# Attention's probabilities times values: one fp32 product against three 16-bit products, with low parts made on GpSimd and VectorE

## The chip, the cores and the metric

The kernel runs on one core of a Trainium2 chip. The metric is the device time of one execution in microseconds, lower is better.

## The reference, cut to what matters

```python
# x: (32 images, 128 channels, 32 x 32), so N = 1024 positions of C = 128
def L0(x):                                    # global attention, one head, per image
    h = group_norm(x, 32 groups)
    q, k, v = split(qkv_w @ h + qkv_b)
    attn = softmax((q^T k) * C ** -0.5)       # 1024 x 1024
    return x + proj_w @ (v @ attn^T) + proj_b
x = L0(x)
t = tokens(x)                                 # (32, 1024, 128)
t = t + L1_attn(layernorm(t))                 # windows of 32, 8 heads of 16, then an MLP of 4 x 128, layer norms
t = t + L1_ffn(layernorm(t))                  # input and weights rounded to fp8, one product, bias
```

The change is in `v @ attn^T` of the first stage.

## The kernel before, in words

Each engine runs its own list of steps per turn of a loop over images. The lists stand in `PROGRAM` (line 46) as text: `pv:3-` is step pv with index 3 for the image one behind the turn's, `--` two behind, and `@5` on TensorE's list gives the PSUM bank. The order is fixed by hand or by a planner outside the file; the engines meet only through semaphores. `iterations` (line 115) gives the turns: the first four and the last two are written out, the 28 between are a hardware loop (`Fori`, line 285). `tenants` and `claim` make TensorE wait until the last holder of a bank has been read; `RELEASE` (line 96) says by which semaphore.

An image's global attention goes like this. `qg`, `kg` and `vg` (lines 902 to 916) make queries, keys and values from three 16-bit products each (`three`, line 868: high x high, high x low, low x high). The values come with the output projection folded in. `max` (line 926) is a rough product of the high parts whose row maxima VectorE takes (line 705); the maxima go through `shift` to be subtracted inside the score product. `st` (line 947), c = 0 to 15, makes the transposed scores of 128 keys x 512 queries; the half of the queries is c // 8, the key tile c % 8. ScalarE turns a score tile into p with one exponential (line 524), into a ring of four fp32 buffers `p32` (`PRING = 4`). `pv` (line 961) multiplies the four 128-query tiles of that p, as the stationary operand, with 128 x 129 values `vg32`; column 129 is ones and gives the row sum. Eight of these accumulate in two PSUM banks; VectorE then divides and adds x (line 735).

```python
last = mm(ps[:, b, at:at + PVW], p32[:, c % PRING, part], vg32[:, j, :], start=j == 0 and q % 2 == 0,
          stop=j == MT - 1, skip_group_check=True)
```

The second stage works on two halves of 512 tokens: `turn_in`, `q`, `k`, `v`, `score0`/`score1` (line 1022), softmax per window, `pv0`/`pv1` (line 1040), `out`, `turn_mid`, `up0` to `up3`, `down` (line 1072, fp32), then the third stage with `turn_q` and `ffn`. A high part is a copy to fp16 by ScalarE, its low part a subtraction by VectorE (lines 699, 760, 765, 774, 807). Layer norms take their statistics on VectorE (lines 742 to 751), the power of -0.5 on GpSimd (line 380), and the scaling on ScalarE (line 493). GpSimd also does softmax's product (line 414), rounding (422, 424) and sums with rows (398 to 440). SyncE issues the transfers that spread keys and probabilities (lines 323, 330).

## Time and profile before

| | us |
|---|---|
| three runs | 2353.22, 2352.03, 2344.88 |
| median | 2352.03 |
| the profiled execution, its own time | 2352.98 |
| its span in the profile | 2351.2 |

The profiled execution is one more run of the same program, and all rows come from it. Engines are PE (TensorE; PEld is its weight loads, which overlap), DVE (VectorE), ACT (ScalarE), POOL (GpSimd), SP (SyncE). A matmul's duration includes its way through the array, so that the price of one in a stream is the distance from its start to the next start. A group's name is output <- inputs; L976 is line 976.

### The profile page before, as it was taken

How to read it: one execution, taken by the hardware profiler on the slowest of the kernel's cores; microseconds unless marked ns; L12 is line 12 of the kernel's file. 1: busy time of each engine (PE TensorE's matmuls, PEld its weight loads, DVE VectorE, ACT ScalarE, POOL GpSimd, SP SyncE). 2: the span in 40 equal slices, each digit the busy share in tenths (PEclk: the TensorE clock that was granted, in tenths of full speed). 3: DMA queues.
4: the chain of work that ended last, by engine and by line, in shares of the span. 5: the costliest groups of instructions: out<-in, count | busy, mean ns of one | idle time of the engine just before them, and what ended most of it. 6: DMA issues, size and time to landing. Idle time of an engine off the chain costs nothing.

```text
span 2351.2 us, 62343 instructions
## 1 busy us (share of the span) xinstructions
PE 2205.4 (94%) x21902; PEld 1605.7 (68%) x21902; DVE 1753.6 (75%) x5668; ACT 1480.0 (63%) x2881; POOL 1229.4 (52%) x1323
## 2 busy tenths in 40 slices
PE   4999999999999999999999999999999999999984
PEld 3677766677776677776677776677777677767663
DVE  5677777777787777787777787777787787787753
ACT  2566666766666766666666666666666666666653
POOL 5255554555554555554555555555555555555544
PEclk8999999999999999999999999999999999999997
DMA  1111111111111111111111111111111111111110
GB/s 44 35 31 33 42 36 45 38 33 29 44 36 45 38 33 30 42 36 45 41 31 33 39 36 45 42 29 35 36 36 45 44 28 36 35 36 45 36 28 19
DMA packets 76094, 86.08 MB, mean 37 GB/s; under 512 B 20624, under 2 KB 55440, under 8 KB 76048
## 3 DMA queue, kind: packets, MB, share of 16 engines
q1 hardware_dynamic: 62368, 52.44, 9.3%
q10 hardware_dynamic: 13680, 33.04, 4.3%
q8 instruction: 28, 0.46, 0.1%
q14 instruction: 18, 0.15, 0.0%
HBM read 18.29 MB, written 16.78 MB: 15 GB/s over the span
## 4 chain that ended last, share of the span: by engine, by line
PE 72%; DVE 10%; ACT 8%; issue 4%; DMA 3%; SPq 3%; POOL 1%; ACTq 0%; DVEq 0%; POOLq 0%
PE ps L976 15%; PE ps L1072 10%; PE ps L870 9%; PE ps L872 9%; PE ps L871 9%; PE ps L957 4%; PE ps L1040 4%; ACT y L493 3%; PE ps L1022 3%; PE ps L934 2%; PE ps L988 2%; DMA ptbd<-et 2%; PE ps L923 1%; SPq L330 1%; SPq L323 1%
## 5 line engine op out<-in xcount | busy, mean ns | idle before, releaser
L380 POOL TENSOR_TENSOR rstd<-veps,halfpow 128x4 f32<-128x4 f32 x256 | 264.5, 1033 | 531.6 <-DVE veps L750 531.6
L976 PEld LDWEIGHTS ps<-vg,p 128*128 128x128 f32 x4096 | 505.6, 192 | 40.4 <-ACT p L524 6.5
L976 PE MATMUL ps<-vg,p 128*128 128x129 f32 x4096 | 523.2, 277 | 0.9 <-ACT p L524 0.9
L524 ACT ACTIVATE p<-ps 128x512 f32<-128x512 f32 x512 | 291.9, 589 | 128.1 <-PE ps L872 104.3
L705 DVE TENSOR_REDUCE cm<-ps 128x1 f32<-128x512 f32 x512 | 334.7, 680 | 16.2 <-PE ps L934 16.1
L414 POOL TENSOR_TENSOR e<-e,srec 128x512 f32<-128x512 f32 x128 | 134.3, 1049 | 243.2 <-DVE srec L793 240.2
L1072 PE MATMUL ps<-w,hid 128*128 128x128 f32 x2048 | 241.7, 276 | 1.7 <-ACT hid L576 1.7
L1072 PEld LDWEIGHTS ps<-w,hid 128*128 128x128 f32 x2048 | 236.2, 192 | 7.6 <-issue 1.8
L576 ACT ACTIVATE hid<-ps,cols 128x512 f32<-128x512 f32 x256 | 165.8, 684 | 97.7 <-PE ps L872 97.7
L934 PE MATMUL ps<-kgh,qgh 128*128 128x512 f16 x512 | 176.0, 384 | 40.6 <-DVE qgl L699 34.1
L957 PE MATMUL ps<-shift,minus 128*128 128x512 bf16 x512 | 194.5, 380 | 2.0
L870 PE MATMUL ps<-qgh,kgh 128*128 128x512 f16 x512 | 194.5, 380 | 0.0
L871 PE MATMUL ps<-qgl,kgh 128*128 128x512 f16 x512 | 194.4, 380 | 0.0
L872 PE MATMUL ps<-qgh,kgl 128*128 128x512 f16 x512 | 194.3, 379 | 0.0
L567 ACT ACTIVATE oh<-ps 128x512 f16<-128x512 f32 x64 | 38.2, 597 | 175.5 <-PE ps L1040 175.5
L398 POOL TENSOR_TENSOR y<-y,rows 128x512 f32<-128x512 f32 x64 | 81.6, 1275 | 127.4 <-PE ps L988 127.4
L760 DVE TENSOR_TENSOR xl<-ps,xh 128x512 f16<-128x512 f32 x128 | 88.5, 692 | 72.7 <-ACT xh L532 69.5
L824 DVE TENSOR_TENSOR w<-ps,res 128x512 f32<-128x512 f32 x64 | 44.3, 692 | 130.0 <-PE ps L1072 126.9
L1040 PE MATMUL ps<-ptbd,v 128*32 128x128 f32 x4096 | 134.3, 278 | 4.8 <-DMA ptbd<-et 3.3
L493 ACT ACTIVATE y<-y,nshift,rstd 128x128 f32<-128x128 f32 x256 | 105.2, 483 | 43.2 <-POOL nshift L387 43.2
L493 ACT ACTIVATE y<-t,nshift,rstd 128x128 f32<-128x128 f32 x256 | 105.5, 483 | 39.2 <-POOL nshift L387 20.1
L1040 PEld LDWEIGHTS ps<-ptbd,v 128*32 128x32 f32 x4096 | 107.5, 111 | 29.0 <-DMA ptbd<-et 22.6
(184 smaller groups left out, 5508.6 us busy)
## 6 DMA issues: line engine op xcount, KB each, us to landing
ptbd<-et SPq DMA_DIRECT2D x512, 64.0 KB, 2.1
kbd<-kk SPq DMA_DIRECT2D x512, 32.0 KB, 2.0
out_y<-o_sb ACTq DMA_DIRECT2D x64, 256.0 KB, 2.4
x_sb<-in_x ACTq DMA_DIRECT2D x31, 512.0 KB, 3.9
x_sb<-in_x SPq DMA_DIRECT2D x1, 512.0 KB, 3.4
e<-in_w_t SPq DMA_DIRECT2D x1, 256.0 KB, 3.7
w<-in_w_t SPq DMA_DIRECT2D x1, 256.0 KB, 3.7
hid<-in_in_w_t SPq DMA_DIRECT2D x1, 192.0 KB, 2.4
```

The lines of the kernel that those rows point to most:

```text
L380: g.tensor_tensor(rstd[:, k, h, :], veps[:, k, h, :], halfpow[:], ALU.pow).then_inc(s[f"ln_pow{k}"], 1)
L493: last = sc.activation(dst[:, h, P * j:P * (j + 1)] if dst is z else dst[:, h, j, :], src[:, h, j, :], ACT.Identity, bias=nshift[:, k, h, ...
L524: sc.activation(p32[:, c % PRING, :], bank("st", c), ACT.Exp, scale=C ** -0.5).then_inc(s["p_made"], 1)
L705: v_.reduce_max(cm[:, c // 2, c % 2:c % 2 + 1], bank("max", c), X).then_inc(s["max_out"], 1)
L870: mm(dst, lhi, rhi, start=first, stop=False, **kw)
L871: mm(dst, lhi, rlo, start=False, stop=False, **kw)
L872: return mm(dst, llo, rhi, start=False, stop=last, **kw)
L934: mm(bank("max", c), qgh[:, P * (c // 2):P * (c // 2 + 1)], kgh[:, HALF * (c % 2):HALF * (c % 2 + 1)], start=True, stop=True).then_inc(s[" ...
L957: mm(bank("st", c), minus[:], shift[:, h, :], start=True, stop=False)
L976: last = mm(ps[:, b, at:at + PVW], p32[:, c % PRING, part], vg32[:, j, :], start=j == 0 and q % 2 == 0, stop=j == MT - 1, skip_group_check ...
L1040: last = mm(ps[WIN * two:WIN * (two + 1), BANK["pv0", h], P * j:P * (j + 1)], v32[:, h, odd, j, WIN * two:WIN * (two + 1)], ptbd[:, h, j, ...
L1072: last = mm(bank("down", h)[:, part], hid[:, f, part], w2[:, f, :], start=f == 0, stop=f == FT - 1)
```

## The change

- pv's product is three products of 16-bit operands with the same accumulation: upper half of p x high part of vg, upper half x low part, low part x high part. The upper half is read in place: every second 16-bit word of `p32`, seen as bf16. The low part `p_lo` (fp16, a ring of four as well) is p32 minus that upper half; GpSimd makes it for c % 4 in (0, 2), VectorE for the others, in steps called `st` on their lists.
- ScalarE writes vg as fp16 (`vgh`), VectorE adds a step `vg` for the low part (`vgl`, bf16). Bank vg is released by the low part. Ones stay in column 129 of vgh, zeros in that of vgl.
- pv waits for the low part's semaphore instead of p's.
- The lists of all five engines are laid out anew, with new banks. The main loop is written out turn by turn instead of a hardware loop.

In the diff, ScalarE's and SyncE's lists are cut.

```diff
+LOW_POOL = (0, 2)
...
     "pe": """
-        max:1@1- max:2@2- max:3@0- vg:1@5- turn_in:1@3-- pv0:0@1-- max:4@2- max:5@5- k:1@4-- max:6@0- pv1:0--
-        max:7@3- turn_x:0@4- v:1@5-- out:0@2-- q:1@1-- shift:0@0- turn_x:1@3- max:8@2- st:0@4- max:9@0- st:1@3-
-        max:10@2- pv:0- score0:1@0-- max:11@5- turn_mid:0@3-- st:2@4- score1:1@0-- up0:0@2-- up1:0@3-- pv:1-
-        up2:0@2-- up3:0@1-- st:3@3- st:4@0- down:0@2-- pv0:1@0-- pv1:1-- max:12@1- st:5@5- max:13@3- max:14@2-
-        out:1@4-- st:6@0- pv:2- pv:3- st:7@1- max:15@3- pv:4- pv:5- shift:1@4- turn_mid:1@2-- pv:6- pv:7- up0:1@1--
-        up1:1@0-- up2:1@4-- up3:1@3-- st:8@5- gn1:0@4 down:1@2-- pv:8- st:9@0- turn_in:0@1- st:10@5- st:11@0- k:0@2-
-        turn_q:0@1-- st:12@3- pv:9- st:13@4- ffn:0@2-- q:0@1- st:14@0- pv:10- gn2:0@2 pv:11- st:15@2- pv:12-
-        score0:0@1- score1:0@3- pv:13- pv:14- pv:15- vg:0@5 kg:0@3 kg:1@4 qg:0@2 turn_q:1@0-- v:0@5- qg:1@1
-        ffn:1@0-- max:0@5""",
+        qg:1@0- vg:1@2- turn_in:1@1-- v:0@4-- max:2@3- max:3@5- k:1@1-- max:4@4- max:5@0- pv0:0@3-- max:6@5- pv1:0--
+        max:7@2- turn_x:1@1- q:1@0-- max:8@5- out:0@3-- shift:0@2- v:1@4-- st:0@2- st:1@0- score0:1@1-- score1:1@5--
+        st:2@3- max:9@2- max:10@4- turn_mid:0@1-- st:3@0- pv:0- max:11@5- up0:0@1-- up1:0@3-- up2:0@0-- up3:0@1--
+        st:4@4- down:0@0-- pv0:1@3-- pv1:1-- pv:1- pv:2- out:1@5-- st:5@1- max:12@4- max:13@3- max:14@5- st:6@2-
+        pv:3- st:7@1- max:15@3- pv:4- pv:5- turn_mid:1@0-- pv:6- shift:1@1- pv:7- up0:1@4-- st:8@0- up1:1@3--
+        gn1:0@5 up2:1@4-- up3:1@0-- st:9@1- down:1@5-- st:10@0- st:11@3- turn_in:0@2- pv:8- st:12@4- turn_q:0@5--
+        k:0@2- q:0@3- pv:9- pv:10- st:13@4- st:14@1- pv:11- gn2:0@2 st:15@5- pv:12- ffn:0@4-- score0:0@1-
+        score1:0@2- pv:13- kg:0@5 pv:14- pv:15- kg:1@2 qg:0@0 turn_x:0@4 turn_q:1@1-- vg:0@5 ffn:1@1-- max:0@1
+        max:1@4""",
     "dve": """
-        ln_in:1-- turn_p0:0-- turn_p1:0-- qg:0- qg:1- max:0- kg:0- max:1- max:2- kg:1- turn_in:1-- max:3- max:4-
-        max:5- k:1-- max:6- pv1:0-- max:7- maxima:0- out:0-- max:8- max:9- q:1-- max:10- score0:1-- turn_mid:0--
-        prob0:1-- score1:1-- turn_p0:1-- prob1:1-- turn_p1:1-- max:11- down:0-- pv1:1-- max:12- out:1-- max:13-
-        max:14- max:15- maxima:1- gn0:0 turn_mid:1-- ln_q:0-- pv:7- ln_in:0- quant:0-- down:1-- turn_in:0- gn1:0
-        k:0- ln_q:1-- q:0- gn2:0 quant:1-- score0:0- score1:0- prob0:0- pv:15- prob1:0-""",
+        pv:15-- kg:0- ln_in:1-- qg:0- turn_p0:0-- kg:1- max:0- vg:0- turn_p1:0-- max:1- qg:1- turn_in:1-- vg:1-
+        max:2- max:3- k:1-- max:4- max:5- max:6- max:7- pv1:0-- maxima:0- q:1-- out:0-- max:8- score0:1-- score1:1--
+        prob0:1-- turn_mid:0-- prob1:1-- turn_p0:1-- max:9- max:10- st:1- turn_p1:1-- gn0:0 max:11- down:0-- pv1:1--
+        st:3- out:1-- max:12- max:13- max:14- st:5- max:15- maxima:1- st:7- turn_mid:1-- ln_q:0-- pv:7- ln_in:0-
+        gn1:0 quant:0-- down:1-- turn_in:0- st:9- k:0- st:11- ln_q:1-- st:13- q:0- gn2:0 st:15- quant:1-- score0:0-
+        score1:0- prob0:0- prob1:0-""",
...
     "pool": """
-        prob1:1-- keep:1-- norm_mid:0-- down:0-- out:1-- norm_out:0-- norm_mid:1-- ln_q:0-- ln_in:0- quant:0--
-        down:1-- norm_out:1-- bias_out:0- ln_q:1-- gn2:0 quant:1-- prob0:0- prob1:0- ln_in:1- bias_out:1- keep:0-
-        out:0- prob0:1-""",
+        out:0-- st:0- bias_out:1-- prob0:1-- prob1:1-- norm_mid:0-- keep:0-- st:2- down:0-- st:4- keep:1-- out:1--
+        st:6- norm_out:0-- norm_mid:1-- ln_q:0-- st:8- ln_in:0- quant:0-- down:1-- st:10- norm_out:1-- st:12-
+        ln_q:1-- gn2:0 st:14- quant:1-- prob0:0- prob1:0- ln_in:1- bias_out:0-""",
...
 RELEASE = {
-    "qg": ("qg_lo", 2, False), "kg": ("kg_lo", 2, False), "vg": ("vg_made", 2, False),
+    "qg": ("qg_lo", 2, False), "kg": ("kg_lo", 2, False), "vg": ("vg_lo", 2, False),
     "turn_x": ("xt_made", 2, False), "max": ("max_out", 2 * MT, False), "shift": ("shift_made", 2, False),
...
         kgh, kgl = sb("kgh", [P, N], F16), sb("kgl", [P, N], F16)
-        vg32 = sb("vg32", [P, MT, PVW])
+        vgh, vgl = sb("vgh", [P, MT, PVW], F16), sb("vgl", [P, MT, PVW], BF16)
         cm = sb("cm", [P, MT, 2])
         p32 = sb("p32", [P, PRING, HALF])
+        p_lo = sb("p_lo", [P, PRING, HALF], F16)
+        p_hi = p32[:].bitcast(BF16)[:, :, 1::2]
         rsum = sb("rsum", [P, 2, 2])
...
             x_in x_bias gn_stats gn_mv gn_mm gn_mean gn_diff gn_var gn_veps gn_pow gn_scale gn_neg gn_coef h32_made h_hi h_lo
-            qg_mm kg_mm vg_mm turn_x_mm qg_hi kg_hi vg_made qg_lo kg_lo xt_made
+            qg_mm kg_mm vg_mm turn_x_mm qg_hi kg_hi vg_made vg_lo qg_lo kg_lo xt_made
             max_mm max_out cmax_made chi_made cparts_made shift_turned shift_made
-            st_mm p_made pv_mm rsum_made t_made
+            st_mm p_made p_low_pool p_low_dve pv_mm rsum_made t_made
             turn_in_mm turn_mid_mm x_hi x_lo q_mm k_mm v_mm
...
+        def low_by(c):
+            return "pool" if c % 4 in LOW_POOL else "dve"
+        def low_count(img, c):
+            each = [low_by(x) == low_by(c) for x in range(2 * MT)]
+            return upto(img, sum(each[:c + 1]), per=sum(each))
         def by_head(ap):
...
                 iteration(i, i)
-            with engine.Fori(loop.start, loop.stop) as i:
+            for i in loop:
                 iteration("steady", i)
...
                                 pattern=[[GROUP, P // GROUP], [0, GROUP]], channel_multiplier=-1).then_inc(s["const_mask"], 1)
-                for tile, value in ((cparts[:], 0.0), (vg32[:], 1.0), (ones, 1.0), (shift[:], 0.0)):
+                for tile, value in ((cparts[:], 0.0), (vgh[:], 1.0), (vgl[:], 0.0), (ones, 1.0), (shift[:], 0.0)):
                     g.memset(tile, value).then_inc(s["const_made"], 1)
...
+            def st(kind, img, c):
+                pool.wait_ge(s["p_made"], upto(img, c + 1, per=2 * MT))
+                if due(value := upto(img, c + 1 - PRING, per=2 * MT)):
+                    pool.wait_ge(s["pv_mm"], value)
+                at = c % PRING
+                g.tensor_tensor(p_lo[:, at, :], p32[:, at, :], p_hi[:, at, :], ALU.subtract).then_inc(s["p_low_pool"], 1)
             def quant(kind, img, h):
...
-            run(pool, "pool", {"gn2": gn2, "ln_in": power_step(0), "out": power_step(1), "bias_out": bias_out, "norm_mid": norm_mid, "keep": keep, "prob0": prob(0), "prob1": prob(1), "quant": quant, "down": power_step(2), "norm_out": norm_out,
+            run(pool, "pool", {"gn2": gn2, "st": st, "ln_in": power_step(0), "out": power_step(1), "bias_out": bias_out, "norm_mid": norm_mid, "keep": keep, "prob0": prob(0), "prob1": prob(1), "quant": quant, "down": power_step(2), "norm_out": norm_out,
                        "ln_q": power_step(3)}, prologue)
...
                 if isinstance(img, int) and img == 0 and c == 0:
-                    act.wait_ge(s["const_made"], 9)
+                    act.wait_ge(s["const_made"], 10)
                     act.wait_ge(s["pv_mm"], value)
-                sc.activation(vg32[:, HT * c:HT * (c + 1), 0:C], tiles(bank("vg", c)), ACT.Copy).then_inc(s["vg_made"], 1)
+                sc.activation(vgh[:, HT * c:HT * (c + 1), 0:C], tiles(bank("vg", c)), ACT.Copy).then_inc(s["vg_made"], 1)
...
                 if isinstance(img, int) and img == 0:
-                    act.wait_ge(s["const_made"], 9 + 2 * (1 + HEADS + HT))
+                    act.wait_ge(s["const_made"], 10 + 2 * (1 + HEADS + HT))
                 src = bank("v", h).rearrange("p (b c) -> p b c", c=2 * HD)
...
                 dve.wait_ge(s["weights_in"], 16 * 18)
-                dve.wait_ge(s["const_made"], 9)
+                dve.wait_ge(s["const_made"], 10)
                 dve.wait_ge(s["const_mask"], 4)
...
                 return step
+            def vg(kind, img, c):
+                dve.wait_ge(s["vg_made"], upto(img, c + 1, per=2))
+                here = slice(HT * c, HT * (c + 1))
+                v_.tensor_tensor(vgl[:, here, 0:C], tiles(bank("vg", c)), vgh[:, here, 0:C], ALU.subtract).then_inc(s["vg_lo"], 1)
...
+            def st(kind, img, c):
+                dve.wait_ge(s["p_made"], upto(img, c + 1, per=2 * MT))
+                if due(value := upto(img, c + 1 - PRING, per=2 * MT)):
+                    dve.wait_ge(s["pv_mm"], value)
+                at = c % PRING
+                v_.tensor_tensor(p_lo[:, at, :], p32[:, at, :], p_hi[:, at, :], ALU.subtract).then_inc(s["p_low_dve"], 1)
             def quant(kind, img, h):
...
             run(dve, "dve", {"gn0": gn0, "gn1": gn1, "gn2": gn2, "qg": global_lo("qg", qgh, qgl, QGB),
-                      "kg": global_lo("kg", kgh, kgl, KGB), "max": row_max,
-                      "maxima": maxima, "pv": pv, "ln_in": ln_in,
+                      "kg": global_lo("kg", kgh, kgl, KGB), "vg": vg, "max": row_max,
+                      "maxima": maxima, "st": st, "pv": pv, "ln_in": ln_in,
                       "turn_in": turned_lo("turn_in", "x_hi", "x_lo"), "q": q, "k": k, "score0": score(0),
...
                         pe.wait_ge(s["t_made"], value)
-                    pe.wait_ge(s["vg_made"], upto(img, 2, per=2))
-                pe.wait_ge(s["p_made"], upto(img, c + 1, per=2 * MT))
+                    pe.wait_ge(s["vg_lo"], upto(img, 2, per=2))
+                pe.wait_ge(s["p_low_" + low_by(c)], low_count(img, c))
                 for q in range(HT):
-                    last = mm(ps[:, b, at:at + PVW], p32[:, c % PRING, part], vg32[:, j, :], start=j == 0 and q % 2 == 0,
-                              stop=j == MT - 1, skip_group_check=True)
+                    last = three(ps[:, b, at:at + PVW], p_hi[:, c % PRING, part], p_lo[:, c % PRING, part], vgh[:, j, :], vgl[:, j, :],
+                                 first=j == 0 and q % 2 == 0, last=j == MT - 1, skip_group_check=True)
                 last.then_inc(s["pv_mm"], 1)
```

## Rows read from the trace of the kernel before

**Rows 1.** The page: span, busy time, share and count of instructions of each engine
```profile
span 2351.2 us, 62343 instructions
PE 2205.4 (94%) x21902; PEld 1605.7 (68%) x21902; DVE 1753.6 (75%) x5668; ACT 1480.0 (63%) x2881; POOL 1229.4 (52%) x1323
```
**Rows 2.** The chain of work, "down" of the first half: start us, us, what
```profile
115.07 3.57 PE ps L1072 x32
...
185.53 3.57 PE ps L1072 x32
...
256.28 3.57 PE ps L1072 x32
...
328.12 3.57 PE ps L1072 x32
...
1244.10 3.57 PE ps L1072 x32
...
1314.52 3.57 PE ps L1072 x32
```
**Rows 3.** One period: us, then PE, PEld, DVE, ACT, POOL busy, PEclk, DMA, GB/s
```profile
1202.42:1272.84 70.42, 68.17 (x686) 49.80 (x685) 54.17 (x176) 46.13 (x91) 37.62 (x40) 1.00 0.14 37
```
**Rows 4.** Longest wait of PE in that period: us in total, times, longest
```profile
PE ps L934 <- DVE qgl L699: 1.1, 1, 1.1
```
**Rows 5.** Weight loads by form, whole run: busy us, mean ns | idle before
```profile
L976 PEld LDWEIGHTS ps<-vg,p 128*128 128x128 f32 x4096 | 505.6, 192 | 40.4 <-ACT p L524 6.5 <-issue 0.9 <-DVE t L735 0.7
...
L1040 PEld LDWEIGHTS ps<-ptbd,v 128*32 128x32 f32 x4096 | 107.5, 111 | 29.0 <-DMA ptbd<-et 22.6 <-issue 2.0 <-DVE cm L705 0.3
...
L1022 PEld LDWEIGHTS ps<-kbd,qh 128*32 128x32 f16 x2048 | 46.5, 96 | 30.2 <-DVE e L783 14.0 <-issue 5.9 <-DMA kbd<-kk 1.7
...
L872 PEld LDWEIGHTS ps<-wh,hl 128*128 128x128 f16 x256 | 25.3, 99 | 0.0
```
**Rows 6.** Timeline of PE: start us, us, instruction
```profile
1206.78 1.05 PE L976 MATMUL ps<-vg,p 128*128 128x129 f32 x8
1207.67 0.28 PE L900 MATMUL ps<-gtmp,group_mean 128*128 128x1 f32 x2
...
1209.65 1.05 PE L976 MATMUL ps<-vg,p 128*128 128x129 f32 x8
1210.64 0.40 PE L1022 MATMUL ps<-kbd,qh 128*32 128x256 f16 x8
...
1212.06 2.95 PE L976 MATMUL ps<-vg,p 128*128 128x129 f32 x24
1214.84 0.22 PE L870 MATMUL ps<-wh,hh 128*128 128x128 f16 x1
...
1215.51 0.38 PE L870 MATMUL ps<-hh,wh 128*128 128x512 f16 x1
...
1255.48 1.95 PE L976 MATMUL ps<-vg,p 128*128 128x129 f32 x16
1257.27 0.39 PE L942 MATMUL ps<-identh,cparts 128*128 128x128 bf16 x4
```
**Rows 7.** VectorE: groups by form, then two rows of its timeline
```profile
L646 DVE TENSOR_TENSOR w1l<-e,w1h 128x512 bf16<-128x512 f32 x1 | 0.7, 691 | 0.0
...
1212.25 0.69 DVE L783 TENSOR_TENSOR e<-ps,smax 128x512 f32<-128x512 f32 x1
1212.86 0.68 DVE L781 TENSOR_REDUCE smax<-ps 128x16 f32<-128x512 f32 x1
```
**Rows 8.** GpSimd: groups by form
```profile
L424 POOL TENSOR_TENSOR qz<-z,expo 128x512 bf16<-128x512 f32 x64 | 81.5, 1273 | 5.0
```
**Rows 9.** Timeline of VectorE and GpSimd
```profile
1264.44 1.18 POOL L380 TENSOR_TENSOR rstd<-veps,halfpow 128x4 f32<-128x4 f32 x1 [1.42 <-DVE veps L750]
1265.15 0.43 DVE L837 TENSOR_SCALAR z<-z 128x512 f32<-128x512 f32 x1 [0.72 <-ACT z L493]
...
1269.85 1.02 POOL L380 TENSOR_TENSOR rstd<-veps,halfpow 128x4 f32<-128x4 f32 x1 [0.64 <-DVE veps L750]
```

12 lines of the change are left out of this document (6 added, 6 removed).

## The prediction

> **What bounds the kernel now.** I read the head of the page first: TensorE is busy for 94% of the span, VectorE for 75%, ScalarE for 63%, GpSimd for 52% [rows 1]. A mean over stages can mislead, so I looked for the period. The fp32 "down" products of an image's first half start at 1244.10 and again at 1314.52 us: one image takes 70.42 us in the middle of the run [rows 2]. 32 periods are 2253 of the 2351.2 us; the other 98 are the filling and emptying of the software pipeline. In one whole period TensorE is busy for 68.17 of 70.42 us at a granted clock of 1.00, VectorE for 54.17, ScalarE for 46.13, GpSimd for 37.62 [rows 3]. The waits of TensorE in that period are few and short; the longest is 1.1 us for a low part that VectorE makes [rows 4]. So TensorE's own instructions set the period, and what is taken from them shortens it as long as nobody else becomes late. VectorE has 16.25 us of slack per period (70.42 - 54.17), GpSimd 32.8, ScalarE 24.3.
>
> **TensorE: three 16-bit products for one fp32 product.** One pv step multiplies four 128-query tiles. In fp32 each tile is two instructions, so a step is eight [rows 5]. The timeline gives the real price, which is the distance between starts, not the duration: three steps take 1214.84 - 1212.06 = 2.78 us, two take 1257.27 - 1255.48 = 1.79, a single one 0.89 (1207.67 - 1206.78), and one with the narrow score tiles behind it 0.99 (1210.64 - 1209.65) [rows 6]. These seven steps are 6.45 us, 0.92 each; 16 of them are 14.7 us of an image's 70.42.
>
> After the change a step has 12 instructions of 129 columns with 16-bit operands. The same kind stands right behind, with 128 columns: the first of twelve starts at 1214.84, what follows them at 1215.51, so 0.67 us for twelve, 0.056 each [rows 6]. One column more adds under 1%. The mixture of fp16 on one side and bf16 on the other is in those twelve already (line 871), at the same pace. So a step costs 0.67 and 16 of them 10.8 us: 3.9 us less per image, 32 x 3.9 = **125 us less** over the run.
>
> **What the trace does not show: a strided weight load.** The upper halves of p are read in place, every second 16-bit word. All 16-bit weight loads in the trace are of adjacent words: 98 or 99 ns, as against 192 ns for fp32 [rows 5]. From below, a strided load costs what an adjacent one does and hides behind its matmul; nothing suggests that it could be cheaper. From above, it is as slow as an fp32 one, whose pairs follow each other at 0.112 us (2.78 / 24) [rows 6]. I take the lower end, since a 16-bit load of 32 columns takes as long as one of 128 (96 and 99 ns) [rows 5]: four times the words cost nothing, so reading words is not what such a load spends its time on. An fp32 load falls from 192 to 111 ns with a quarter of the columns [rows 5], so there it is. The other end is a rival below.
>
> **VectorE's additions.** Per image, eight subtractions of 512 columns for the odd c and two for the low part of vg. The one two-input operation on SBUF of that size took 691 ns [rows 7]; from start to start such operations follow at 0.61 (1212.86 - 1212.25) [rows 7]. Ten of them are 6.1 us. Slack after: period 66.5 (70.42 - 3.9), less 54.2, less 6.1 = 6.2 us, 9% where it was 23%. In itself that is hidden, but it is the cover of every high/low pair that TensorE waits for, and all steps stand in one fixed order.
>
> **GpSimd's additions.** Eight subtractions at 1.27 us [rows 8] are 10.2 us; that makes 47.8 of 66.5 us busy, and 19 idle. What is behind them in its queue are normalisation steps: each power of four numbers (1.02 us [rows 9]) that VectorE and ScalarE wait for can now stand up to 1.3 us behind a subtraction that itself waits for p. The new order spaces them; I cost them at nothing, with VectorE's slack as cover.
>
> **The longer path of p.** Before, TensorE waited for the exponential; now it waits for exponential and subtraction, 0.7 to 1.3 us later, in a ring of four buffers that now three engines hold. In the steady order other steps stand between st and pv of the same c every time (pv:0 comes after st:3, pv:7 six steps after st:7), so it is covered. In the filling of the pipeline it is not; that is some 2 us once, and I leave it in the range. ScalarE writes vgh in fp16 in place of fp32: same size, same price. The bank of vg is freed one 0.69 us operation later; the new order has eight other steps ahead of the bank's next tenant.
>
> **Unrolling.** The main loop becomes straight code on every engine. Turns 0 to 3 and the last two were straight code before. From the first "down" of turn 2 to that of turn 3 it is 70.46 us (185.53 - 115.07), inside the loop 70.42 (1314.52 - 1244.10); the step into the loop (256.28 - 185.53 = 70.75) and its first turn back (328.12 - 256.28 = 71.84) cost 1.8 us more, once [rows 2]. So straight code gains at most that. More instructions must be brought in, beside transfers that keep the DMA engines 14% busy [rows 3]; the straight turns showed no lack. I take zero.
>
> **The new waits.** TensorE idles 2.25 us of a period now (70.42 - 68.17), with VectorE idle for 23%. If such waits grow in inverse proportion to VectorE's slack (23% to 9%), they become 5.7, 3.5 more per image; if the re-laid order absorbs the additions, 0 more, or even some of the 2.25 disappears. I take a third of the upper end, 1.1 us per image, 35 us in all, because a subtraction's place is free within the ring of four, so that it can lie in one of VectorE's present holes; the part that remains is for the pairs where it can't.
>
> **Sum**, against the profiled execution: 2352.98 - 125 + 35 = 2263; the median of the three runs, 2352.03, is 1 us below that execution, so **2262 us**. With no new waits 2227, with all of them 2338. A measurement here tells 0.5% (12 us) from no change.
>
> **Rival A: the shared read path of VectorE and GpSimd makes VectorE the bound.** What the rows show: a two-port VectorE operation and a GpSimd operation that overlap do disturb each other. The power at 1264.44 took 1.18 us, while VectorE began on z at 1265.15; one at 1269.85 took 1.02 [rows 9]. No row shows a VectorE operation with two SBUF inputs beside a long GpSimd operation. If each of the eight subtractions must wait for a GpSimd operation in flight, that is 0.72 (the 47.8 of 66.5 us) x half of 1.27 = 0.46 us, 3.7 per image. VectorE then needs 54.2 + 6.1 + 3.7 = 64.0 us, and with even half of its present idle pattern kept (4 us) the period is 68 to 69: 2352 - 32 x 1.9 = **about 2295**, range 2285 to 2335. The Trainium skill states the rule ("SBUF — State Buffer", Who interferes with whom): a VectorE instruction with two SBUF inputs and a GpSimd instruction that reads SBUF exclude each other for the whole instruction. By that rule the trace agrees in direction only: the overlap seen cost GpSimd 0.16 us, and VectorE no time that shows in its 0.43 us. Chance 22%.
>
> **Rival B, slower: the strided weight load binds.** Place: the eight of twelve loads in a step that read p in place. Price at the fp32 spacing: 8 x 0.112 + 4 x 0.056 = 1.12 us a step against 0.92 now, 0.20 more, times 512 = +102 us, with a little new waiting **about 2455**. It decides from the point where a strided load needs more than (0.92 - 0.22) / 8 = 87 ns of its own. For it: a word in two is read in vain, and fp32 loads of the same span take twice as long. Against it: the 32-column comparison above. Chance 9%.
>
> **Rival C: gain eaten to nothing.** Rival A's contention together with a fixed order in which late subtractions push the powers of four normalisations: the period stays at about 70.4, **2340 to 2365**. Chance 4%.
>
> **Rival D: more than I count.** The new order also removes TensorE's present waits, 1 to 2 us per image: **2165 to 2215**. Chance 7%.
>
> **How the numbers follow.** My case (2215 to 2285) 58%, A 22%, B 9%, C 4%, D 7%. The range 2215 to 2325 holds the first and most of A, about 80%. Faster by over 0.5% (below 2340): 58 + 22 + 7 less a little = 86%; within 0.5%: 4%; slower: 10%.
>
> **What would show it.** Right: the period of "down" products 66.5 to 68 us; twelve 129-column products in 0.67 us; weight loads of p at line 976's successor near 99 ns; VectorE near 60 us per period; subtractions at 0.69 and 1.27. Rival A: those subtractions on VectorE longer than 0.75 us or late without a waiting signal, GpSimd operations stretched. Rival B: 129-column products of upper halves 0.09 us or more apart. Wrong altogether: waits for instruction fetch inside the period, or a granted clock below 1.00.

## The result, and the profile after

The changed kernel is **slower: 2565.3 us** (median; 2556.4 to 2568.3) against 2352.6, a ratio of **1.091, 95% interval 1.088 to 1.095**. The forecast of 2262 is wrong in sign, and 2565 lies outside its range. The profiled execution took 2562.8 us, its span is 2561.0.

The page, as [rows 1], and the longer of the two queues that bring instructions (packets, MB, share):

```profile
span 2561.0 us, 63875 instructions
PE 2158.9 (84%) x23950; PEld 1483.6 (58%) x23950; DVE 2086.5 (81%) x5988; ACT 1494.8 (58%) x2881; POOL 1564.2 (61%) x1580
...
q8 instruction: 193, 3.16, 0.5%
```

The same 1000 us from the middle of the run, first of before, then of after (us, then PE, PEld, DVE, ACT, POOL busy, PEclk):

```profile
900.00:1900.00 1000.00, 968.78 (x9681) 708.67 (x9679) 770.11 (x2517) 655.67 (x1281) 535.49 (x571) 1.00 0.14 37
```
```profile
900.00:1900.00 1000.00, 859.81 (x9556) 592.15 (x9555) 831.45 (x2383) 601.14 (x1159) 614.78 (x615) 0.98 0.13 35
```

The period, read off ScalarE's instruction that writes hh once per image: 14 starts of before, 13 of after (duration in ns, then first and last start):

```profile
L459 ACT ACTIVATE hh<-x_sb,gtmp x14: 1224/1226/1227, 928.2 to 1843.7; 128x1024 f16<-128x1024 f32 x14
```
```profile
L479 ACT ACTIVATE hh<-x_sb,gtmp x13: 1225/1227/1232, 926.4 to 1863.3; 128x1024 f16<-128x1024 f32 x13
```

(1843.7 - 928.2) / 13 = 70.42 us before and (1863.3 - 926.4) / 12 = 78.1 after. Every period in what follows is read this way.

The prices of TensorE's instructions came out as forecast. One pv step, as [rows 6], and the three weight loads, as [rows 5]:

```profile
1270.81 0.22 PE L903 MATMUL ps<-vgh,p 128*128 128x129 f16 x1
1270.86 0.22 PE L904 MATMUL ps<-vgl,p 128*128 128x129 bf16 x1
...
1271.49 0.38 PE L967 MATMUL ps<-kgh,qgh 128*128 128x512 f16 x1
```
```profile
L904 PEld LDWEIGHTS ps<-vgl,p 128*128 128x128 bf16 x2048 | 204.2, 100 | 23.9
L905 PEld LDWEIGHTS ps<-vgh,p_lo 128*128 128x128 f16 x2048 | 203.7, 99 | 0.0
L903 PEld LDWEIGHTS ps<-vgh,p 128*128 128x128 bf16 x2048 | 203.2, 99 | 107.4 <-DVE p_lo L863 55.1 <-POOL p_lo L436 20.6 <-issue 10.2
```

Twelve products take 0.68 us, and the load that skips every second word costs 99 ns like the adjacent one. So the loss isn't there. TensorE was freed, and waits (us in total, times, longest; the 1000 us above):

```profile
PE ps L1055 <- DMA kbd<-kk: 47.0, 25, 2.8
PE ps L903 <- DVE p_lo L863: 17.5, 26, 0.9
PE ps L903 <- DVE e L808: 15.4, 13, 1.4
```

VectorE and GpSimd by group, as [rows 7, 8] (busy us, mean ns):

```profile
L863 DVE TENSOR_TENSOR p_lo<-p 128x512 f16<-128x512 f32 x256 | 250.2, 977 | 1.1 <-ACT p L544 0.7 <-issue 0.4
L872 DVE TENSOR_SCALAR expo<-z 128x512 int32<-128x512 int32 x64 | 84.1, 1315 | 2.2
L436 POOL TENSOR_TENSOR p_lo<-p 128x512 f16<-128x512 f32 x256 | 276.1, 1079 | 29.3 <-ACT p L544 24.8 <-PE ps L905 4.3 <-issue 0.2
L457 POOL TENSOR_TENSOR w<-w,rows 128x512 f32<-128x512 f32 x64 | 95.2, 1487 | 21.6 <-ACT w L513 21.6
L874 DVE TENSOR_SCALAR expo<-expo 128x512 f32<-128x512 f32 x64 | 49.9, 780 | 2.2
```

The two exponent instructions of the quantization, which the change doesn't touch, took 427 ns in the kernel before:

```profile
L841 DVE TENSOR_SCALAR expo<-expo 128x512 f32<-128x512 f32 x64 | 27.3, 427 | 2.2
L839 DVE TENSOR_SCALAR expo<-z 128x512 int32<-128x512 int32 x64 | 27.3, 427 | 2.2
```

After, VectorE's timeline and GpSimd's show how one grew:

```profile
1238.43 0.68 DVE L863 TENSOR_TENSOR p_lo<-p 128x512 f16<-128x512 f32 x1
1239.03 0.42 DVE L870 TENSOR_SCALAR z<-z 128x512 f32<-128x512 f32 x1
1239.48 2.40 DVE L872 TENSOR_SCALAR expo<-z 128x512 int32<-128x512 int32 x1
```
```profile
1239.47 2.12 POOL L387 TENSOR_TENSOR hl<-h,hh 128x1024 f16<-128x1024 f32 x1 [2.45 <-DVE h L713]
```

A GpSimd instruction that began 0.01 us earlier holds VectorE for 2 us: the two end within 0.3 us of each other. VectorE's share of such waiting over the run is 256 x (0.977 - 0.68) = 76 us on the subtractions, 56.8 and 22.6 us on the two exponent instructions (84.1 and 49.9 less 27.3 each): 155 us, where [rows 9] showed none. The layer norms' variance step of four columns (`veps`) adds 15.6 us: 256 of them take 59.1 us, 43.5 before.

### The profile page after: what moved, and what is told of

Same layout as the page of the kernel before. It is cut to its first block and busy times, and to the rows that moved or that the text cites. A ratio compares the mean times of both kernels' runs of the same rounds, so it can differ in the third digit from the quotient of the medians.

```text
span 2561.0 us, 63875 instructions
## 1 busy us (share of the span) xinstructions
PE 2158.9 (84%) x23950; PEld 1483.6 (58%) x23950; DVE 2086.5 (81%) x5988; ACT 1494.8 (58%) x2881; POOL 1564.2 (61%) x1580
## 3 DMA queue, kind: packets, MB, share of 16 engines
q8 instruction: 193, 3.16, 0.5%
## 5 line engine op out<-in xcount | busy, mean ns | idle before, releaser
L903 PE MATMUL ps<-vgh,p 128*128 128x129 f16 x2048 | 380.3, 224 | 46.9 <-DVE p_lo L863 40.4
L904 PE MATMUL ps<-vgl,p 128*128 128x129 bf16 x2048 | 378.9, 223 | 0.0
L905 PE MATMUL ps<-vgh,p_lo 128*128 128x129 f16 x2048 | 378.7, 223 | 0.0
L436 POOL TENSOR_TENSOR p_lo<-p 128x512 f16<-128x512 f32 x256 | 276.1, 1079 | 29.3 <-ACT p L544 24.8
L903 PEld LDWEIGHTS ps<-vgh,p 128*128 128x128 bf16 x2048 | 203.2, 99 | 107.4 <-DVE p_lo L863 55.1
L863 DVE TENSOR_TENSOR p_lo<-p 128x512 f16<-128x512 f32 x256 | 250.2, 977 | 1.1 <-ACT p L544 0.7
L904 PEld LDWEIGHTS ps<-vgl,p 128*128 128x128 bf16 x2048 | 204.2, 100 | 23.9
L905 PEld LDWEIGHTS ps<-vgh,p_lo 128*128 128x128 f16 x2048 | 203.7, 99 | 0.0
L967 PE MATMUL ps<-kgh,qgh 128*128 128x512 f16 x512 | 164.8, 383 | 28.5 <-ACT o_sb L609 23.4
L582 ACT ACTIVATE e<-e 128x512 f32<-128x512 f32 x128 | 80.2, 626 | 183.5 <-DVE e L808 183.4
```

The lines of the kernel that those rows point to most:

```text
L436: g.tensor_tensor(p_lo[:, at, :], p32[:, at, :], p_hi[:, at, :], ALU.subtract).then_inc(s["p_low_pool"], 1)
L863: v_.tensor_tensor(p_lo[:, at, :], p32[:, at, :], p_hi[:, at, :], ALU.subtract).then_inc(s["p_low_dve"], 1)
L903: mm(dst, lhi, rhi, start=first, stop=False, **kw)
L904: mm(dst, lhi, rlo, start=False, stop=False, **kw)
L905: return mm(dst, llo, rhi, start=False, stop=last, **kw)
L967: mm(bank("max", c), qgh[:, P * (c // 2):P * (c // 2 + 1)], kgh[:, HALF * (c % 2):HALF * (c % 2 + 1)], start=True, stop=True).then_inc(s[" ...
```

## The experiments

The theories after the result: **CONTENTION** (VectorE and GpSimd lock each other out), **LOAD** (VectorE has too much in a stiff order), **ORDER** (the re-laid lists themselves cost), **FETCH** (the written-out program costs), and later **LOOP**: TensorE's order was never the only bound; another chain that comes round once per image is nearly as long. Each ratio is to the kernel before, and the period is us per image from 900 to 1900 us.

### One part of the change at a time

Written out alone:

```diff
-            with engine.Fori(loop.start, loop.stop) as i:
+            for i in loop:
```


> The kernel before with its main loop written out turn by turn, nothing else. Theory CONTENTION (the changed kernel is slow because the new subtractions and GpSimd's operations exclude each other on SBUF): this run is as the kernel before, 2345 to 2355 us, period of the down products 70.4 us. Theory ORDER (the new lists are slow in themselves): the same. Rival FETCH (instructions of 32 written-out turns arrive late): a good part of the 212 us appears here, 2400 us or more.

**2380.0 us, ratio 1.012 (1.011 to 1.014).** Writing out costs 28 us, more than the two first theories allowed and far less than FETCH expected. Periods that were 70.4 throughout now lie between 69.95 and 74.1, with one of 75.9 later.

The changed kernel's lists with the arithmetic of before (32-bit products, no low parts), written out:

```diff
-  last = three(ps[...], p_hi[...], p_lo[...], vgh[...], vgl[...], ...)
+  last = mm(ps[...], p32[...], vg32[...], ...)
```


> The changed kernel's lists on all engines and its written-out loop, with the arithmetic of before: pv as one fp32 product, no low parts on GpSimd or VectorE. Theory CONTENTION: without the subtractions the lists run about as before, 2340 to 2400 us, and VectorE's operations on expo go back to about 430 ns. Theory ORDER: the lists lose time without any subtraction, 2480 us or more, with the same waits of TensorE on the key transfers as in the changed kernel.

**2446.2 us, 1.040 (1.038 to 1.042),** between the two forecasts: the lists cost 66 us more than writing out does, and the exponent instructions are at 427 and 428 ns. An order that makes room for work may be worse while the work is absent, so in the changed kernel ORDER may cost less than these 66; no run shows how much.

The changed kernel without the low parts of p (two products per tile; low p times high v is left out):

```diff
-  last = three(..., p_hi, p_lo, vgh, vgl)
+  mm(to, p_hi, vgh); last = mm(to, p_hi, vgl)
```


> The changed kernel without the low parts of p: no subtractions on either engine, two products per tile instead of three (the product low p x high vg is left out). Theory CONTENTION: the period falls by the 9 us per image of stretching and waiting and by 0.22 x 16 = 3.6 us of TensorE, to some 65 us, 2150 to 2200 us. Theory ORDER: TensorE's 3.6 us are hidden by waits, the period stays above 72 us, 2400 us or more.

**2406.3 us, 1.023 (1.021 to 1.025),** where CONTENTION expected 2150 to 2200. Against the run above, TensorE has 16 x 0.47 = 7.5 us less to do per image, VectorE the low part of the values more, and 40 us of the 241 show. The 16 subtractions, with the third product that uses them and the longer path of p, are the other 159 of 2565.

The lists of before, with the changed arithmetic and the subtractions put in by hand:

```diff
-  max:10- score0:1--      (dve)
+  max:10- st:1- score0:1--
```


> The lists of before with the changed arithmetic: vg's low part and nine subtractions put into VectorE's holes (c odd, and 14), seven on GpSimd, pv:0 one step later; written out. Theory CONTENTION: the subtractions collide here too, slower than before, 2400 us or more. Theory ORDER: 2250 to 2340 us, faster than before.

**2684.5 us, 1.141 (1.139 to 1.144).** TensorE waits 80.7 us in 1000 for VectorE's low parts. My placing was poor (and one subtraction more went to VectorE, nine and seven); it shows only that the re-laid lists are better than naive ones for this work.

### Contention or load

In each, the changed kernel with one edit. First, VectorE's subtraction becomes a reduction of the same slot, one operand (its low parts are zero):

```diff
-  v_.tensor_tensor(p_lo[:, at, :], p32[:, at, :], p_hi[:, at, :], ALU.subtract)
+  v_.reduce_max(pmax[:, at:at + 1], p32[:, at, :], X)
```


> The changed kernel with one edit: where VectorE subtracted the upper half of p from p (two operands from on-chip memory), it now takes the row maximum of the same slot of p into a spare column, one operand, same waits, same place in its list; its slots of the low part stay zero, so the low part of odd or even tiles that VectorE made is left out. TensorE still does all twelve products. CONTENTION (an instruction of VectorE with two operands from on-chip memory waits for GpSimd's running one, and stretches it): the 8 instructions per image fall from 0.98 us to about 0.6 whether GpSimd is busy or not, GpSimd's stretched ones (1.45 to 1.49) fall back part of the way towards 1.27, and the run falls from 2565 to 2450 to 2510 us. LOAD (VectorE simply has 8 more instructions in a stiff order): 2550 to 2570 us. Above 2520 speaks against CONTENTION as the main cause.

The whole steady part in the hardware loop again:

```diff
-            for i in loop:
+            with engine.Fori(loop.start, loop.stop) as i:
```


> The changed kernel with its 30 steady images in the hardware loop again instead of written out; nothing else. If the cost of the written-out program is the 28 us that it had on the kernel before, 2530 to 2545 us. If it grows with the length of the list, or with the engines that have less slack now (FETCH is a larger share of the loss): 2480 to 2520. If it hides behind the new waits (the engines wait for each other anyway): 2555 to 2570.

GpSimd's subtraction narrowed to one column, then VectorE's:

```diff
-  g.tensor_tensor(p_lo[:, at, :], p32[:, at, :], p_hi[:, at, :], ...)
+  g.tensor_tensor(p_lo[:, at, 0:1], p32[:, at, 0:1], p_hi[:, at, 0:1], ...)
```


> The changed kernel with GpSimd's 8 subtractions per image narrowed to one column (the low part of its tiles of p is left out, apart from one column), waits and places kept. VectorE's 8 stay whole. CONTENTION: two operands of VectorE still meet GpSimd's other work (37.6 us of 70 busy before), but not these 8 x 1.04 us, so about a quarter of the stretch goes: 2490 to 2530 us. If GpSimd's subtractions are the late link by themselves (TensorE waits for them, GpSimd's tail runs late): 2440 to 2490. If VectorE's half alone makes the loss: 2545 to 2565.

> The changed kernel with VectorE's 8 subtractions per image narrowed to one column (the low part of its tiles left out), waits and places kept; GpSimd's 8 stay whole. It frees VectorE of 8 x 0.98 us and the one port of 8 long claims. CONTENTION and LOAD both say faster; what tells is the distance to the one-operand run: CONTENTION says that run already holds most of the gain, so this one lies only 0 to 40 us below it, at 2440 to 2490; LOAD says the whole gain comes here: 2430 to 2480 while the one-operand run stays at 2550 or more.

| run | us | ratio, interval | against 2565 |
|---|---|---|---|
| VectorE one operand | 2465.0 | 1.049 (1.043 to 1.054) | -100 |
| hardware loop | 2516.4 | 1.071 (1.068 to 1.074) | -49 |
| GpSimd narrowed | 2556.1 | 1.088 (1.084 to 1.091) | -9 |
| VectorE narrowed | 2427.1 | 1.033 (1.028 to 1.038) | -138 |

The one-operand run's VectorE and GpSimd:

```profile
L864 DVE TENSOR_REDUCE pmax<-p 128x1 f32<-128x512 f32 x256 | 173.0, 676 | 1.9 <-ACT p L545 1.6 <-issue 0.2
...
L458 POOL TENSOR_TENSOR w<-w,rows 128x512 f32<-128x512 f32 x64 | 81.6, 1275 | 25.6 <-ACT w L514 25.6
```

The instruction reads the same 512 columns in the same place and takes 676 ns on average, never stretched (660 to 687), and GpSimd's 1487 are 1275 again. Trading the second operand, and the write of 512 columns that went with it, gives 100 us back, inside what CONTENTION expected; LOAD expected next to nothing. The 38 us more of the narrowed run can't be put down to LOAD, so how much of the loss is LOAD stays open. The unchanged exponent instruction is blocked in the one-operand run and nearly free in the narrowed one, 48 us of VectorE's time between them:

```profile
L875 DVE TENSOR_SCALAR expo<-expo 128x512 f32<-128x512 f32 x64 | 77.3, 1207 | 2.2
```
```profile
L874 DVE TENSOR_SCALAR expo<-expo 128x512 f32<-128x512 f32 x64 | 29.2, 456 | 2.2
```

With VectorE narrowed to one column, that one column still lasts 430 ns on average, half of them 156 or less and the longest 1242:

```profile
L863 DVE TENSOR_TENSOR p_lo<-p 128x1 f16<-128x1 f32 x256 | 110.1, 430 | 1.9 <-ACT p L544 1.6 <-issue 0.3
```

The long ones stand behind a running GpSimd instruction, and end with it, as if they were 512 columns wide:

```profile
1145.27 1.24 DVE L863 TENSOR_TENSOR p_lo<-p 128x1 f16<-128x1 f32 x1
```
```profile
1145.19 1.29 POOL L460 TENSOR_TENSOR u<-u,w 128x512 f32<-128x512 f32 x1
```

GpSimd's half cost next to nothing (the third of my three forecasts): VectorE's subtractions still take 896 ns and one exponent instruction 1285, since VectorE runs into GpSimd's other instructions.

If so, all 16 on GpSimd should be best:

```diff
-LOW_POOL = (0, 2)
+LOW_POOL = (0, 1, 2, 3)
```
(st:1, st:3, ... moved from VectorE's list to GpSimd's, each beside its neighbour; hardware loop)

> The changed kernel in the hardware loop with all 16 subtractions per image on GpSimd, none on VectorE; to be set beside the changed kernel in the hardware loop (2516). VectorE loses 8 x 0.94 us and its two-operand claims; GpSimd gains 8 x 1.04 and goes to about 65 us of busy time in 100. CONTENTION: 2380 to 2440 us, since narrowing VectorE's half gave 138 back and GpSimd's half weighs only 9. If GpSimd's stiff list is now the late one (TensorE waits for its parts of p): 2450 to 2520. Above 2520 CONTENTION would need another explanation.

**2702.3 us, 1.151 (1.148 to 1.154): a miss,** above the 2520 from which I had said that CONTENTION would need another explanation. The period is 81.9, and TensorE waits for GpSimd:

```profile
PE ps L895 <- POOL p_lo L436: 65.0, 36, 4.4
PE ps L895 <- POOL hl L387: 25.9, 12, 2.2
```

GpSimd is busy only 64 us in 100, but its list is stiff, and with two subtractions in a row each stands before something that others need. So this run says nothing for or against CONTENTION. Another placing wasn't tried.

### What TensorE's saving is worth

The kernel before, its own lists and loop, two 16-bit products (low p left out), VectorE making only the low part of the values:

```diff
+  ... prob0:0- pv:15- prob1:0- vg:0      (dve)
+  ... kg:1- turn_in:1-- vg:1- max:3-     (dve)
```


> The kernel before with its own lists and its hardware loop; probabilities times values as two 16-bit products per tile (upper 16 bits of p read in place, times the upper and the low part of the values), so 8 instructions of TensorE at 0.056 us per tile of p in place of 8 at 0.11; VectorE makes the low part of the values (2 x 0.69 us per image) and nothing else is added. The low part of p is left out. It joins what the runs so far left standing of the change (TensorE's saving) with none of what they charged (written-out program, new lists, subtractions of p). TensorE drops by 16 x (0.92 - 0.45) = 7.5 us per image. If TensorE's order bounds the kernel as it did before: 2352 - 32 x 7.5 = 2112, and as VectorE gets 1.4 us more and other waits come up, 2150 to 2260 us. If the kernel before was already near the waits of the other engines (the lists' stiffness, as the run without the low parts hints: 2406 on the new lists): 2300 to 2360 us.

**2356.0 us, 1.003 (1.002 to 1.005).** Nothing of the change is charged but VectorE's 1.4 us, TensorE is 5.7 us per image less busy (68.2 to 62.5), and there is no gain:

```profile
900.00:1900.00 1000.00, 883.42 (x9650) 594.21 (x9651) 782.43 (x2527) 655.76 (x1276) 531.31 (x569) 1.00 0.14 37
```

Here the chain of waits gives the first hint. First before, then this run:

```profile
PE 72%; DVE 10%; ACT 8%; issue 4%; DMA 3%; SPq 3%; POOL 1%; ACTq 0%; DVEq 0%; POOLq 0%
PE ps L976 15%; PE ps L1072 10%; PE ps L870 9%; PE ps L872 9%; PE ps L871 9%; PE ps L957 4%; PE ps L1040 4%; ACT y L493 3%; PE ps L1022 3%; PE ps L934 2%; PE ps L988 2%; DMA ptbd<-et 2%; PE ps L923 1%; SPq L330 1%; SPq L323 1%
```
```profile
PE 37%; DVE 31%; issue 10%; POOL 7%; ACT 6%; SPq 1%; DMA 1%; DVEq 0%; ACTq 0%; POOLq 0%
PE ps L1089 9%; PE ps L886 6%; PE ps L888 5%; PE ps L887 5%; DVE stats L758 4%; DVE cm L721 4%; PE ps L1057 3%; POOL rstd L391 3%; PE ps L973 2%; ACT y L504 2%; DVE mv L763 2%; DVE smax L797 2%; DVE kgl L710 2%; PE ps L950 2%; DVE ssum L807 2%
```

In the chain of before the pv products (L976) hold 15%. As soon as they are cheaper, another chain of nearly the same length, through "down", VectorE's statistics and GpSimd's powers, is the longest. The pv products (L993 and L994 there) aren't among its 15 largest lines; they hold 15 us, under 1% (L973 is the first product of `st`). Two tests: the saving with nothing on VectorE, and VectorE's addition with no saving.

```diff
-  vg32 = sb("vg32", [P, MT, PVW])            p32 = sb("p32", [P, PRING, HALF])
+  vg32 = sb("vg32", [P, MT, PVW], F16)       p32 = sb("p32", [P, PRING, HALF], F16)
```


> The kernel before with the tiles of p and of the values declared 16-bit (ScalarE writes them so), one product per tile: 4 instructions of TensorE at 0.056 us in place of 8 at 0.11; no other instruction is changed, none added. The low parts of both are left out. TensorE does 16 x (0.92 - 0.22) = 11.2 us less per image. The run with two products took 6.2 us less of TensorE per image and came out at 2356, no faster. EATEN (VectorE's two new instructions per image, 1.4 us, and the wait for them ate it there; TensorE's order is the bound): here nothing eats it, 2000 to 2200 us. LOOP (a loop of dependences through VectorE, GpSimd and the rest of TensorE, that comes round once per image, lasts about 70 us whatever these products cost): 2300 to 2355 us.

```diff
+  v_.tensor_tensor(vgl[:, here, 0:C], tiles(bank("vg", c)), vg32[:, here, 0:C], ALU.subtract)
-  pe.wait_ge(s["vg_made"], upto(img, 2, per=2))
+  pe.wait_ge(s["vg_lo"], upto(img, 2, per=2))
```


> The kernel before with VectorE's low part of the values alone (2 x 0.69 us per image, where the run with two products had it), written to a tile that nobody reads, and TensorE's first product with the values waiting for it; the 32-bit products of before stay, so nothing of the result is changed. VectorE was idle 23 us in 100. If TensorE's order is the bound and VectorE has slack: 2345 to 2360 us. LOOP (VectorE's stretch from the quantization to the last key is part of the loop): 1.0 to 1.4 us per image, 2380 to 2400 us, and then TensorE's saving in the run with two products was worth about 30 us and no more.

**2388.6 us, 1.017 (1.015 to 1.020)** for one product per tile: 10 us less of TensorE per image (58.2 us busy where it was 68.2), and slower, above both forecasts. **2385.1 us, 1.016 (1.013 to 1.018)** for VectorE's 1.4 us, as LOOP expected: period 71.6 from 70.4. VectorE, idle 23 us in 100, has no slack there. Part of this is a direct wait: TensorE waits 11 us in 1000, 0.8 per image, for this very low part, because it also frees a bank.

The one-product kernel's periods alternate, 69.7 and 73.7. Two neighbours (us, busy times as above, then the granted clock, the seventh figure):

```profile
1153.89:1227.58 73.69, 62.27 (x614) 40.08 (x620) 54.37 (x177) 46.10 (x92) 37.01 (x40) 0.93 0.13 36
1227.58:1297.26 69.68, 58.17 (x614) 38.13 (x620) 54.26 (x177) 46.07 (x91) 37.38 (x40) 1.00 0.14 38
```

So even at the full clock, with TensorE idle for 11.5 us, an image takes 69.7. The slow ones have a stretch like this:

```profile
1200.00:1205.00 5.00, 2.27 (x23) 1.50 (x21) 4.18 (x13) 3.19 (x7) 4.84 (x5) 0.86 0.00 0
1205.00:1210.00 5.00, 4.81 (x12) 1.73 (x12) 3.48 (x24) 2.21 (x4) 2.71 (x6) 0.50 0.00 0
```

TensorE was busy 2.27 of 5 us, the clock fell to 0.50 (1.2 in place of 2.4 GHz), and the twelve products of the next 5 us took all of it. Each product made twice, on the same 16-bit tiles (numerator and row sum double, their quotient stays), gives TensorE work back and VectorE none:

```diff
+  mm(ps[...], p32[...], vg32[...], start=..., stop=False)
   last = mm(ps[...], p32[...], vg32[...], start=False, stop=...)
```


> The 16-bit kernel of the run before (ScalarE writes p and the values 16 bits wide, low parts left out) with each product made twice into the same bank: numerator and row sum both double, so the quotient stays. TensorE gets 0.45 us per tile of p, as with two products, and VectorE nothing. CLOCK (the run with one product fell to a granted clock of 0.50 in part of its images because TensorE idled too much, and that cost it what the rest gave): clock back to 1.00, period at the 69.4 to 69.8 us of that run's undisturbed images, 2310 to 2330 us. If something else made that run slow (TensorE's slack moves the order of releases, say): 2370 to 2390 again. TENSOR BOUND after all: 2352 - 32 x 7.5, 2110 to 2150.

VectorE's four low parts of the global projections narrowed to one column, on the kernel before; then both edits:

```diff
+  part = slice(part.start, part.start + 1)
   v_.scalar_tensor_tensor(lo[:, part], bank(name, c)[:, 0:1], ...)
```


> The kernel before, 32-bit products and all, with VectorE's low parts of the two global projections narrowed to one column (4 instructions of about 0.7 us per image; those low parts are left out), in the stretch where TensorE waits for them. It frees VectorE of some 2.4 us per image. BOTH (TensorE's order and the loop through VectorE tie at about 70 us, so that neither's saving alone shows): TensorE's 68.2 us busy is the floor, 68.5 to 69.8 us per image, 2290 to 2335 us. If VectorE's loop alone is the bound: 68.0 or less, 2275 or less. If VectorE has slack: 2345 to 2355.

> Both edits together: 16-bit p and values with each product made twice, and VectorE's four low parts narrowed. BOTH: more than the sum of the two alone, since each takes away the other's floor: 67.0 to 68.5 us per image, 2240 to 2290 us. If the two savings only add: within 10 us of 2352 minus the two single gains. If the clock falls (TensorE idle over 10 us in 70): 2300 or more with a granted clock under 0.97.

| run | us | ratio, interval | period |
|---|---|---|---|
| each product twice | 2351.4 | 0.999 (0.998 to 1.000) | 69.7 to 71.0 |
| VectorE relieved | 2353.7 | 1.000 (0.999 to 1.001) | 70.4 |
| both | 2325.2 | 0.988 (0.987 to 0.990) | 69.6 |

Neither shows alone, both together give 28 us: that fits a tie in kind. But all three times lie outside the forecasts for a clock restored or for a tie, and the second is where "VectorE has slack" had put it. The periods say more. TensorE relieved alone already has images of 69.7:

```profile
1204.09:1273.79 69.70, 62.32 (x684) 41.82 (x684) 54.32 (x177) 46.09 (x92) 37.38 (x40) 1.00 0.14 38
```

That is the 69.7 of the one-product kernel, with 4 us more of TensorE's work in it: between the two amounts of work the image doesn't get shorter. In the other images the clock dips (0.98), and VectorE's relief adds 0.1 us and a clock of 1.00. So what lies under TensorE's order is another bound at 69.6 to 69.7 us, and TensorE's whole saving was worth 0.8 us per image, 26 in all. With VectorE relieved alone, TensorE's wait for it (the one of [rows 4], 15.2 us in the 1000) is gone and the next, 6.6 us before, grows in its place:

```profile
PE ps L989 <- ACT y L493: 19.8, 28, 1.2
```

Last, the run with both edits and the loop shortened where the chain passes GpSimd (the row scale and residual of norm_out reach only one column in this run; the rest of both is left out):

```diff
-  g.tensor_tensor(w[:, h], w[:, h], row(RG2), ALU.mult)
+  g.tensor_tensor(w[:, h, 0, 0:1], w[:, h, 0, 0:1], row(RG2)[:, 0, 0:1], ALU.mult)
-  g.tensor_tensor(u[:, h], u[:, h], w[:, h], ALU.add)
+  g.tensor_tensor(u[:, h, 0, 0:1], u[:, h, 0, 0:1], w[:, h, 0, 0:1], ALU.add)
```


> The kernel with both edits (2325 us, 69.6 us per image, TensorE busy 62.5 of them at a granted clock of 1.00), with GpSimd's two long instructions of norm_out (scale by the row, add the residual; 1.27 us each, two halves per image) narrowed to one column; their effect on the output is left out. The chain of the two-product kernel runs through one half's pair, between 'down' and the next group norm. LOOP (that chain is what lasts 69.6 us): one pair leaves it, about 2 x 1.2 us per image, to 67.2 to 68.4, 2245 to 2285 us, until TensorE's 62.5 or another leg stops it. If GpSimd is not on what binds: 2315 to 2330 us. If the freed time makes TensorE idle enough for its clock to fall: above 2300 with periods that differ.

**2360.8 us, 1.005 (1.003 to 1.006): 36 us slower than the run it started from** and outside every forecast, with 4.6 us less of GpSimd per image. Its VectorE and GpSimd:

```profile
L842 DVE TENSOR_SCALAR expo<-expo 128x512 f32<-128x512 f32 x64 | 85.4, 1335 | 2.2
```
```profile
1214.53 2.14 POOL L375 TENSOR_TENSOR hl<-h,hh 128x1024 f16<-128x1024 f32 x1 [2.27 <-ACT hh L459]
```
```profile
1214.58 2.37 DVE L842 TENSOR_SCALAR expo<-expo 128x512 f32<-128x512 f32 x1
```

and the same pair in the run with both edits:

```profile
1265.81 0.43 DVE L842 TENSOR_SCALAR expo<-expo 128x512 f32<-128x512 f32 x1
```
```profile
1266.03 2.20 POOL L375 TENSOR_TENSOR hl<-h,hh 128x1024 f16<-128x1024 f32 x1 [2.54 <-ACT hh L459]
```

There VectorE was first by 0.22 us and lost nothing; here GpSimd is first by 0.05, and VectorE loses 1.94 us, once in nearly every image: 58 us over the run (85.4 - 27.3). So the test doesn't settle which steps make the 69.6, and it shows the lock in a kernel without a single new subtraction.

### Where writing out costs

SyncE issues the small transfers of keys and probabilities. TensorE's waits for them over the whole run, before and written out:

```profile
PE ps L1022 <- DMA kbd<-kk: 6.7, 6, 3.6
...
PE ps L1040 <- DMA ptbd<-et: 3.3, 4, 1.5
```
```profile
PE ps L1040 <- DMA ptbd<-et: 20.8, 27, 1.9
PE ps L1022 <- DMA kbd<-kk: 19.4, 26, 4.4
```

That is 30 us more, against 28 lost. So SyncE alone went back into the loop:

```diff
+            if key == "sp":
+                with engine.Fori(loop.start, loop.stop) as i: ...
```


> The kernel before with its steady images written out on TensorE, VectorE, ScalarE and GpSimd, but in the hardware loop on SyncE, which issues the 8 + 8 small transfers of keys and probabilities of each half image. ISSUE (what the written-out program costs is SyncE's issuing: single issues of 1.4 and 1.9 us where the loop never had one over 0.60, and TensorE's waits for those transfers rose by 30 us over the run, 3.3 to 20.8 and 6.7 to 19.4, against 28 us lost): 2350 to 2360 us. If the instructions of all engines arrive late: 2370 to 2382, as with everything written out (2380).

> The changed kernel with SyncE alone in the hardware loop. ISSUE: most of the 49 us that the loop on all engines gave back, since there TensorE's waits for keys and probabilities fell from 87.9 + 16.3 to 54.7 + 3.9 us: 2515 to 2530 us. If the other engines' instructions are late as well: 2545 to 2565 us.

**2373.0 us, 1.010 (1.007 to 1.013), and 2560.6 us, 1.090 (1.087 to 1.094).** The forecast of ISSUE falls: SyncE's own written-out program isn't what costs. TensorE's waits for the two transfers stay too, 39 us on the kernel before (40 written out, 10 looped), so late transfers can still be how the time is lost. SyncE's program is short now, and within 80 us its issues for keys still reach 1.74 us (duration in ns, minimum, median and maximum), where none was over 0.60 in the same stretch of the looped kernels:

```profile
L339 SPq DMA_DIRECT2D kbd<-kk x22: 559/589/1740, 1778.3 to 1859.7; - x22
```

From 600 to 2200 us no issue of either transfer takes over 0.69 us in the two looped kernels; in this run the longest take 1.80 and 2.28. Before 600 and after 2200 us the looped kernels too have some of 1.4 to 1.5. The delay comes with the other four engines' written-out programs, which bring 3.16 MB of instructions where the changed kernel in its loop brings 0.49. That these fetches delay SyncE's issues fits the rows, but it was not isolated.

## Why the prediction was wrong, step by step

- **"TensorE's own instructions set the period, and what is taken from them shortens it as long as nobody else becomes late": the step that failed.** That TensorE is busy 68.17 of 70.42 us [rows 3] was read as proof that nothing else is nearly as long. The relieved kernels show a bound at 69.6 to 69.7 us, even with nothing added to any other engine. Of 125 us, 26 were to be had. The chain of waits shows one chain; it is silent on how long the next is. Which steps make the 69.6 stays open.
- **This alone would give no loss, only about 2352 - 26.** The sign comes from the sum's other terms: unrolling and the lists had nothing, the waits behind the subtractions 35 us.
- **The price of twelve products (0.67 us) and of the strided load (99 ns)** were right: 0.68 and 99. Rival B is dead.
- **VectorE's additions, 6.1 us, "In itself that is hidden": wrong twice.** Slack in the sum isn't slack in the place: 1.4 us in the run with VectorE's addition alone cost 1.2 per image. And the subtractions took 0.98 us on average. The price of 0.61 was a distance between starts, taken at an instruction that reads one of its operands from PSUM, the matmul's output memory (`e<-ps,smax`); undisturbed, a subtraction is near it, 0.60 (1239.03 - 1238.43). The missing 0.30 is the waiting.
- **Rival A had the mechanism right and its size wrong.** It gave each subtraction 0.46 us of waiting; measured were 0.30 (0.977 less the undisturbed 0.68). What it left out was the rest of VectorE's list: the exponent instructions of the quantization, one operand each, lost 155 - 76 = 79 us, and five of GpSimd's eight kinds of 1.27 us instruction went to between 1.40 and 1.49. This loss hangs on what meets what: it was 2 us with VectorE's subtractions narrowed, 58 with one operand, and 58 in the run with the shortened loop, which has no new subtraction. The run with one operand gives 100 us back, or 3.1 us per image where the rival said 3.7. Its 2295 was wrong because it took 3.9 us per image of TensorE's saving for granted as well. The reading of [rows 9], "VectorE no time that shows in its 0.43 us", was of a pair in which the overlap was with a power of four columns. The Trainium skill ("SBUF — State Buffer", Who interferes with whom) names both kinds as users of the shared ports, VectorE's with two SBUF inputs and the one-input `tensor_scalar` in a two-port mode, and says that the one that comes first has them for its whole instruction while the other blocks. The numbers here agree: 2.40 us behind a 2.12 us instruction, 0.43 when first.
- **GpSimd's additions at nothing**: narrowing the 8 gave 9 us, so nearly right for 8; with 16 the run is 186 us above the looped kernel.
- **Unrolling at zero: wrong,** 28 us on the kernel before, 49 on the changed one. [Rows 2] compared a few straight turns at the start of a looped program with turns in its loop; they say nothing about 28 more of them, one behind the other. The Trainium skill ("Runtime: NRT & Kernel Launch", Instruction fetch mechanics) calls the cost of crossing a block of instructions "mostly hidden". Here 149 more instruction packets (177 against 28) go with 28 us: 0.19 us each, an estimate that puts the whole loss on them. That no more than this shows per block agrees with the page; the sum over the run does not vanish.
- **The new waits at 35 us** (none "if the re-laid order absorbs the additions"): the lists alone cost 66 us with the old arithmetic, and TensorE's wait for keys went from none of note to 47 us in 1000.
- **The sign of the sum.** From 2352: +28 written out, +66 lists, -40 two products with VectorE's low part of the values, +159 the 16 subtractions with their product, which gives 2565. Each step is measured on top of the ones before it; in another order the shares could differ.

No version that computes all of it beats the kernel before. The fastest, 2325 us, leaves out the low parts of p, of the values and of the global projections.

## What to carry to other kernels

An engine at 97% tells that its order is a bound, not that it is the only one: before pricing a saving, look for a second loop once round per iteration, and test cheaply by deleting the work (here the 16-bit tiles) before building what replaces it. When work moves to VectorE, count what its second operand does to all of GpSimd's long instructions and to VectorE's fast one-operand ones, in both directions, in the places where they meet. In the rows above a start 0.01 or 0.05 us earlier decided who lost 2 us, so that even taking work away can lose time.
